# Moving the softmax scaling behind the value product in a pipelined one-core attention and expert kernel

## The reference, cut to what matters

```python
t = t + attn(ln(t))      # softmax(mask(q k^T * C**-0.5)) v, heads side by side, @ Wp + bp
t = t + ffn(ln(t))       # top 2 of 4 experts, gelu(x w1 + b1) w2 + b2, weighted
```

## Time and profile before

| | |
|---|---|
| median of 3 runs | 470.88 us (469.58, 470.88, 472.49) |
| span of the profiled execution | 469.8 us, 1.1 us under the median |
| mean granted TensorE clock | 0.959 of full speed |
| busy: PE, DVE, ACT, POOL | 429.3, 269.8, 263.7, 146.5 us |
| steady block (1 to 6) | 44.2 us each |

### The profile page before, as it was taken

One profiled execution on the slowest core, in us unless ns is written; L12 is line 12 of the kernel. 1 busy time (PEld: TensorE's weight loads), 2 busy tenths in 40 slices (PEclk: granted clock), 3 DMA queues, 4 the chain that ended last, 5 costly groups with the idle time before them and its releaser, 6 DMA issues.

```text
span 469.8 us, 10623 instructions
## 1 busy us (share of the span) xinstructions
PE 429.3 (91%) x3112; PEld 344.1 (73%) x3112; DVE 269.8 (57%) x954; ACT 263.7 (56%) x740; POOL 146.5 (31%) x309
## 2 busy tenths in 40 slices
PE   6999995449779999999999999999999999999897
PEld 6989994325558767877787787778767877787676
DVE  3888887445523853585277527743763586267424
ACT  2444453236557556664866485568556664866370
POOL 5000000235521542254236215531543254235200
PEclk9999998557979999999999999999999999999999
DMA  8500000031021002100210121012002100210000
GB/s 201 130 0 0 0 0 0 17 71 32 3 57 29 19 0 59 44 17 14 66 38 0 38 51 28 0 46 52 19 0 54 46 0 4 76 22 3 7 11 17
DMA packets 14392, 14.93 MB, mean 32 GB/s; under 512 B 5426, under 2 KB 11412, under 8 KB 14372
## 3 DMA queue, kind: packets, MB, share of 16 engines
q1 hardware_dynamic: 14180, 14.30, 12.1%
q0 software_dynamic: 192, 0.39, 0.3%
HBM read 3.86 MB, written 1.57 MB: 12 GB/s over the span
## 4 chain that ended last, share of the span: by engine, by line
PE 73%; DVE 12%; ACT 5%; issue 5%; SPq 2%; DMA 1%; POOL 1%; DVEq 1%; ACTq 0%; POOLq 0%
PE F L1018 18%; PE T L976 9%; PE A L997 8%; PE F L1034 4%; PE F L1038 4%; PE S L960 4%; PE F L1035 4%; PE S L962 3%; PE F L1014 3%; PE S L965 2%; DVE c L629 2%; DVE ig L627 2%; ACT tc_sb L471 2%; DVE pt_sb L457 1%; PE M L939 1%
## 5 line engine op out<-in xcount | busy, mean ns | idle before, releaser
L406 POOL TENSOR_SCALAR p_sb<-p_sb,rden 128x128 f32<-128x128 f32 (+1 forms) x192 | 79.8, 431 | 135.0 <-DVE rden L710 132.8
L1018 PE MATMUL F<-w_sb,hid 128*128 128x96 f32 x768 | 101.0, 276 | 0.0
L1018 PEld LDWEIGHTS F<-w_sb,hid 128*128 128x128 f32 x768 | 93.4, 192 | 6.0 <-issue 6.0
L518 ACT ACTIVATE p_sb<-S,nmax 128x128 f32<-128x128 f32 (+1 forms) x192 | 78.9, 425 | 17.1 <-DVE nmax L704 17.0
L704 DVE TENSOR_REDUCE nmax<-S 128x2 f32<-128x512 f32 (+1 forms) x80 | 50.7, 634 | 52.7 <-PE S L965 52.3
L457 ACT COPY pt_sb<-T 128x512 f32<-128x512 f32 (+1 forms) x48 | 26.4, 550 | 68.7 <-PE T L976 68.7
L564 ACT ACTIVATE hid<-F,b_sb 128x512 f32<-128x512 f32 x72 | 49.3, 686 | 9.6 <-PE F L1038 9.0
L997 PE MATMUL A<-pt_sb,v_cur 128*32 128x128 f32 x576 | 44.2, 284 | 8.5 <-ACT pt_sb L457 4.5
L976 PE MATMUL T<-id_sb,p_sb 128*128 128x128 f32 x288 | 49.2, 290 | 1.5 <-POOL p_sb L406 1.4
L960 PE MATMUL S<-k_bd,q_st 96*128 96x384 f32 (+2 forms) x96 | 39.3, 416 | 6.5 <-DMA k_bd<-k_cur 6.4
L976 PEld LDWEIGHTS T<-id_sb,p_sb 128*128 128x128 f32 x288 | 30.9, 143 | 16.3 <-issue 13.9
(11 more groups left out here) (140 smaller groups left out, 781.8 us busy)
## 6 DMA issues: line engine op xcount, KB each, us to landing
k_bd<-k_cur SPq DMA_DIRECT2D x96, 32.0 KB, 2.0
q_st<-q_cur SPq DMA_DIRECT2D x28, 96.0 KB, 2.2
k_bd<-k_cur SPq DMA_DIRECT2D x96, 16.0 KB, 1.8
t_st<-t_cm SPq DMA_DIRECT2D x7, 192.0 KB, 2.4
out_y<-y_sb SPq DMA_DIRECT2D x7, 192.0 KB, 1.9
x_pad<-in_x SPq DMA_DIRECT2D x2, 612.0 KB, 8.6
w_sb<-in_w SPq DMA_DIRECT2D x1, 576.0 KB
hid<-in_w SPq DMA_DIRECT2D x1, 576.0 KB, 6.9
```

Source lines behind the costliest of these rows:

```text
L406: last = nc.gpsimd.tensor_scalar(p, p, rden[:, u % 3, i:i + 1], 1.0, ALU.mult, ALU.mult)
L518: last = nc.scalar.activation(p_sb[:, u % 3, i * nk:(i + 1) * nk], S[u % 2][:, i * nk:(i + 1) * nk], ACT.Exp, bias=nmax[:, u % 3, i:i + 1] ...
L1018: last = mm(dst[:, e * C:(e + 1) * C], hid[:, c, s * TT:(s + 1) * TT], w2_sb[:, c], start=False, stop=(c == NCH - 1), skip_group_check=True)
```

## The change

The probabilities stay unscaled. The sums of a query tile's six heads are gathered in den[:, s % 2, :] and inverted once a tile (`recip(n, s)`). POOL spreads the six inverses of a row over 16 columns each (`spread`, 128 x 96); PE multiplies that by the identity (`turn_sums`, an fp32 product into bank M, [96, 128]); ACT copies it to rden_t (`take_spread`); and DVE's `heads_out` writes o_t = A * rden_t. project_out(s) and the uses of M are moved ahead of values in PE's round, EARLY_T0 goes from 1 to 4 and EARLY_XT from 4 to 9.

```diff
-EARLY_T0, EARLY_XT = 1, 4
+EARLY_T0, EARLY_XT = 4, 9
...
-            def scale(n, u):
-                wait_alone(pool, rden_done, NU * n + u + 1)
...
-                for i in range(HG[t]):
-                    p = p_sb[:, u % 3, i * nk:(i + 1) * nk]
-                    last = nc.gpsimd.tensor_scalar(p, p, rden[:, u % 3, i:i + 1], 1.0, ALU.mult, ALU.mult)
-                last.then_inc(scaled, 1)
+            def spread(n, s, first=False):
+                wait_alone(pool, rden_done, 4 * n + s + 1)
+                if s or not first:
+                    wait_alone(pool, spread_ready, 4 * n + s)
+                nc.gpsimd.tensor_copy(rden_c[:], rden[:, s % 2].unsqueeze(2).to_broadcast((128, HEADS, HS))
+                                      ).then_inc(rden_spread, 1)
...
-                scale(n, 0)
                 for j in range(NU):
-                    if j + 1 < NU:
-                        scale(n, j + 1)
+                    for s in range(SPB):
+                        if j + 1 == TILE_END[s]:
+                            spread(n, s, first)
                     if j == EARLY_T0 + 1 and not last:
                         rstd1(n + 1)
...
-            def heads_out(n, s, first=False):
-                act.wait_ge(av_ready, NU * n + TILE_END[s])
-                if s or not first:
-                    act.wait_ge(proj_ready, 4 * n + s)
-                nc.scalar.copy(o_t[:], A[0:C, 0:TT]).then_inc(ot_done, 1)
+            def take_spread(n, s, first=False):
+                act.wait_ge(spread_ready, 4 * n + s + 1)
+                if s or not first:
+                    act.wait_ge(ot_done, 4 * n + s)
+                nc.scalar.copy(rden_t[:], M[0:C, 0:TT]).then_inc(spread_done, 1)
...
                         if j == TILE_END[s]:
-                            heads_out(n, s, first)
+                            take_spread(n, s, first)
+                    if j == EARLY_XT and not last:
+                        take_x1(n + 1)
                     if j in PT_ON_ACT:
                         take_pt(act, n, j, first)
                     if j + 2 < NU:
                         exps(n, j + 2, first)
                     if j == EARLY_T0 and not last:
                         take_t0(n + 1)
-                    if j == EARLY_XT and not last:
-                        take_x1(n + 1)
...
+            def heads_out(n, s, first=False):
+                dve.wait_ge(av_ready, NU * n + TILE_END[s])
+                if s or not first:
+                    dve.wait_ge(proj_ready, 4 * n + s)
+                dve.wait_ge(spread_done, 4 * n + s + 1)
+                V.tensor_tensor(o_t[:], A[0:C, 0:TT], rden_t[:], ALU.mult).then_inc(ot_done, 1)
...
-                    if j + 1 < NU:
-                        recip(n, j + 1)
+                    for s in range(SPB):
+                        if j + 2 == TILE_END[s]:
+                            recip(n, s)
+                        if j == TILE_END[s]:
+                            heads_out(n, s, first)
                     if j not in PT_ON_ACT:
                         take_pt(dve, n, j, first)
-                    if j == EARLY_XT + 1 and not last:
+                    if j == EARLY_XT and not last:
                         x1_rest(n + 1)
...
             def probs_t(n, u, first=False):
-                pe.wait_ge(scaled, NU * n + u + 1)
+                pe.wait_ge(exp_done, NU * n + u + 1)
...
+            def turn_sums(n, s, last=False):
+                if s == 1 and not last:
+                    pe.wait_ge(t0_done, n + 2)
+                elif s == SPB - 1 and not last:
+                    pe.wait_ge(x1lo_done, n + 2)
+                elif s:
+                    pe.wait_ge(t1_done, 4 * n + s)
+                else:
+                    pe.wait_ge(v_done, n + 1)
+                if s == SPB - 1:
+                    pe.wait_ge(t1_done, 4 * n + s)
+                pe.wait_ge(rden_spread, 4 * n + s + 1)
+                mm(M[0:C, 0:TT], rden_c[:].rearrange("p r d -> p (r d)"), id_sb[:], start=True, stop=True
+                   ).then_inc(spread_ready, 1)
...
+                        for s in range(SPB - 1):
+                            if j == TILE_END[s]:
+                                turn_sums(n, s, last)
+                            if j == TILE_END[s] + 1:
+                                project_out(n, s)
+                        if j == EARLY_T0 and not last:
+                            pe.wait_ge(t1_done, 4 * n + 1)
+                            tokens_first(n + 1)
+                        if j == EARLY_XT and not last:
+                            pe.wait_ge(t1_done, 4 * n + 3)
+                            channels_first(n + 1)
                         values(n, j - 1, first)
...
                     project_q(n + 1)
+                turn_sums(n, SPB - 1, last)
                 values(n, NU - 1, first)
```

More of the change, by code:

```diff
@@ L136, in hybrid_kernel @@
         nmax = sb("nmax", [128, 3, HG[0]])
-        den = sb("den", [128, 3, HG[0]])
-        rden = sb("rden", [128, 3, HG[0]])
+        den = sb("den", [128, 2, HEADS])
+        rden = sb("rden", [128, 2, HEADS])
+        rden_c = sb("rden_c", [128, HEADS, HS])
+        rden_t = sb("rden_t", [C, TT])
         p_sb = sb("p_sb", [128, 3, 512])
@@ L197, in hybrid_kernel @@
         av_ready = sem("av_ready")
+        spread_ready = sem("spread_ready")
+        spread_done = sem("spread_done")
+        rden_spread = sem("rden_spread")
         proj_ready = sem("proj_ready")
@@ L235, in hybrid_kernel @@
         comb = sem("comb")
-        scaled = sem("scaled")
         rs1_step = sem("rs1_step")
@@ L280, in as_f32, with row_of @@
             return ap.bitcast(F32)
+        def row_of(h):
+            return 2 * (h % 3) + h // 3
         def queries_taken(eng, n, g):
@@ L397, in residual @@
                                         ALU.add).then_inc(tb_done, 1)
-            def scale(n, u):
-                wait_alone(pool, rden_done, NU * n + u + 1)
-                _, t, _ = UNITS[u]
-                nk = TT * (t + 1)
-                for i in range(HG[t]):
-                    p = p_sb[:, u % 3, i * nk:(i + 1) * nk]
-                    last = nc.gpsimd.tensor_scalar(p, p, rden[:, u % 3, i:i + 1], 1.0, ALU.mult, ALU.mult)
-                last.then_inc(scaled, 1)
+            def spread(n, s, first=False):
[4 more added lines that the diff above has]
+                                      ).then_inc(rden_spread, 1)
             def x1_whole(n):
@@ L514, in exps @@
                     act.wait_ge(pt_ready, NU * n + u - 2)
-                _, t, _ = UNITS[u]
+                a, t, h0 = UNITS[u]
+                s = 2 * a + t
+                if h0 == 0 and (s > 1 or not first):
+                    act.wait_ge(rden_done, 4 * n + s - 1)
                 nk = TT * (t + 1)
@@ L519, in exps @@
                                                 ACT.Exp, bias=nmax[:, u % 3, i:i + 1],
-                                                accum_out=den[:, u % 3, i:i + 1])
+                                                accum_out=den[:, s % 2, row_of(h0 + i):row_of(h0 + i) + 1])
                 last.then_inc(exp_done, 1)
-            def heads_out(n, s, first=False):
-                act.wait_ge(av_ready, NU * n + TILE_END[s])
+            def take_spread(n, s, first=False):
+                act.wait_ge(spread_ready, 4 * n + s + 1)
                 if s or not first:
-                    act.wait_ge(proj_ready, 4 * n + s)
-                nc.scalar.copy(o_t[:], A[0:C, 0:TT]).then_inc(ot_done, 1)
+                    act.wait_ge(ot_done, 4 * n + s)
+                nc.scalar.copy(rden_t[:], M[0:C, 0:TT]).then_inc(spread_done, 1)
             def body(n, first=False, last=False):
@@ L545, in body @@
                         take_t0(n + 1)
-                    if j == EARLY_XT and not last:
-                        take_x1(n + 1)
-                heads_out(n, SPB - 1, first)
+                take_spread(n, SPB - 1, first)
                 if not last:
@@ L705, in row_max, with recip @@
                                 AX.X, ALU.max, negate=True).then_inc(max_done, 1)
[L707 to L710, removed]
+            def recip(n, s):
+                dve.wait_ge(exp_done, NU * n + TILE_END[s])
+                V.reciprocal(rden[:, s % 2], den[:, s % 2]).then_inc(rden_done, 1)
+            def heads_out(n, s, first=False):
[4 more added lines that the diff above has]
+                V.tensor_tensor(o_t[:], A[0:C, 0:TT], rden_t[:], ALU.mult).then_inc(ot_done, 1)
             def attn_residual(n, s, first=False):
@@ L784, in body @@
                     route(n - 1, 1)
-                recip(n, 0)
                 if first:
@@ L812, in body @@
                             normalize2(n, s)
+                heads_out(n, SPB - 1, first)
                 attn_residual(n, SPB - 1)
@@ L1054, in body @@
                     probs_t(n, j, first)
[L1055 to L1075, removed]
                 if not last:
@@ L1081, in body @@
```

(1 more changed line is left out.)

## The result

The changed kernel takes 499.91 us (median of 4 runs, 498.56 to 500.96) against 471.15 (4 runs, 469.58 to 472.49): ratio 1.0603, 95% interval 1.0573 to 1.0634. The profiled execution is the shortest of the four, span 496.7 us. A launch takes about 1.8 us over its span in both kernels (498.56 and 496.7 here; 471.54 and 469.7 in a run of the kernel before).

The account below looks back on a forecast made before the run. TensorE's written order was taken to bound the kernel from block 1 on. Steady blocks 18.4, block 7 0.5 and block 0 2.5 us on the 469.8 span gave 491.2, plus 1.1: 492.3 us, range 486 to 498 (8 in 10: 477 to 503).

Parts of the forecast that it names:

- Bound by TensorE's order, scaling hidden: From block 1 on TensorE's order sets the pace; POOL's scaling is hidden, so removing it can only pay in block 0.
- First wait: Steady block, j = 5: TensorE at turn_sums(1) waits 0.86 us for ACT's copy to t0.
- Second wait: Steady block, j = 7: turn_sums(2) waits 1.75 us for t1 of attn_residual(1), which stands behind normalize1 on DVE.
- Turns: TensorE gets 32 turn_sums at 0.2 us each: 0.8 us a block, 6.4 in all, bounds 4.8 to 7.0.
- Steady term: Blocks 1 to 6 each grow by 3.07 us, from 44.2 to 47.3: 18.4 us in all.
- step 1: Walk of the steady block at j = 4: tokens_first replaces channels_first; probs_t(4) starts at about 205.85, j = 5 at 206.33.
- Block 0: First block: loses POOL's scaling but gets both waits larger, +2.5 us, bounds 0 and +5.
- Block 7's +0.5: Last block, without t0 or normalize1 in the way: 0.8 us of work, part in old waits, so +0.5.
- The clock rival: TensorE may drop to 1.2 GHz in steady blocks, 3 us a block more: 500 to 513 us; chance 0.13.
- Launch around the span: The median of the runs lies 1.1 us over the span, carried over from 491.2 to 492.3 us.
- only work: First rival listed: new waits hidden, some 0.45 us a block added; 472 to 484 us, middle 477; chance 0.15.
- faster: Block 0 loses POOL and DVE links (-4 us), turns fit in steady blocks' old waits (-2.1): 465 us; chance 0.06.

Follow-up runs that it names:

- e5: The kernel before with the softmax scaling left out (no reciprocals on DVE, no multiplies on POOL): 469.22 us, ratio 0.9952.
- e2: The changed kernel with take_t0 put ahead of the exponentials of unit 6 on ACT in round 4: 496.42 us.
- e1: The changed kernel with attn_residual put ahead of norm1 and normalize1 in each of DVE's rounds: 491.58 us.
- e7: e1 with POOL's spread of query tile 2 also one round earlier, ahead of rstd1: 488.53 us.
- e3: The changed kernel with take_t0 as in e2, the spread as in e7, attn_residual as in e1, and normalize1 a round later: 478.93 us, ratio 1.0204.
- e4: The changed kernel with each product of turn_sums issued twice, the second over the first: 507.27 us.
- e8: The changed kernel with ten products that nothing reads issued in block 0 ahead of turn_sums(2), where TensorE otherwise waits: 496.36 us.

## Why the prediction was right, and where it was off

The time lies in the range (477 to 503), the forecast's own 486 to 498 was missed by 2 us, and the growth was 28.8 us where 21.4 were forecast. Step by step, in us from the start of the stretch (189.49 before, 198.15 after):

| start of | forecast | measured |
|---|---|---|
| probs_t(4) | 16.36 | 16.52 |
| turn_sums(1) | 19.11 | 19.35 |
| values(4) | 19.36 | 19.74 |
| turn_sums(2) | 25.16 | 25.46 |
| values(7) | 27.21 | 27.63 |
| project_q | 30.26 | 30.82 |
| project_out(3) | 32.76 | 33.21 |

- **Bound by TensorE's order, scaling hidden.** Right: e5 shows 44.22 us with no scaling at all, and block 0 gives the 2 us.
- **First wait, 0.86 us by t0.** Right in place and releaser; 0.94 as listed, 1.1 from start to start, and e2 took it away and won 1.05.
- **Second wait, 1.75 us by attn_residual behind normalize1.** Right in place, releaser and size (1.53 as listed, 1.7 from start to start). What I did not see is that behind DVE's order stand POOL's (e1) and, once that is mended, heads_out(2) (e7): with M's users in their new places, three queues have to be changed together. e1 alone won 1.02; all together (e3) won 2.37 of the 3.53 us. Of the 1.16 left, 0.86 are the turns (e4).
- **Turns, 0.2 us each.** Right (0.215 in e4). The Trainium skill, page "TensorE: Matmul & The Clock Gate", section "LDWEIGHTS (loading the stationary operand)", would have 80 ns for one load of 96 columns; the trace has 163 ns as the median of these fp32 loads, so that rule does not hold here, while two of them, overlapped with the products, come at the distance of the transposes.
- **Steady term, 3.07 us a block.** Mis-sized: 3.53, in six blocks 2.8 us. A third of it is a slip in step 1: its own terms (+0.2 - 0.28 + 0.28) put probs_t(4) at 206.00, not 205.85, that is at 16.51 from the start of the stretch, where 16.52 was measured; all that follows stood 0.15 too early. The timeline shows the rest: a turn that had to wait takes 0.39 us from its start to the next product's (217.50 to 217.89), and I had counted 0.25, twice; t0's end to the turn's start is 0.13 us, counted as 0.05; project_q comes 0.73 us after probs_t(9), before 0.41, so it waits longer for x1lo than the 0.2 that I gave it. Other pieces came out 0.2 us shorter than walked.
- **Block 0, +2.5 us, bounds 0 and +5.** Mis-sized: +5.45, over its upper bound. The waits in it, 1.51 and 2.33 us, are larger than in the steady blocks, as forecast. The step that failed is the clock: the middle value kept it at its old course, and it fell once more behind the second wait. e8 prices that at 2.7 us; without it the term would be +2.8. Block 7's +0.5 was right (+0.57).
- **The clock rival (0.13).** Not as I had it: the profiled execution has a clock of 1.00 in all steady stretches, and a fall in a steady pass costs 1.3 us where the rival charged 3. The three others have a mean clock of 0.948 against its 0.954 and are 1.2 to 2.4 us longer, and e2, e4 and e8 show single steady stretches that are 1.3 us longer at 0.96 to 0.97. That the same happened in those three executions is inferred, as no trace shows them. By the Trainium skill, page "TensorE: Matmul & The Clock Gate", section "A second HAM failure mode: psum-queue depth-cycling", short idle times between groups can make the clock go up and down. The traces agree in part: every fall in a steady pass comes behind the wait of 1.53 us, and those in the last block behind three or four waits of 0.36 to 0.68 us, but 18 of 24 passes with the long wait kept their clock, and the loop of the kernel before, with two waits of 0.44 and 0.48, never lost it.
- **Launch around the span.** I carried 1.1 us; the runs show 1.8: 0.7 of the miss. With 2.8 from the steady blocks, 2.7 from blocks 0 and 7 and the earlier start, and 1.35 by which the median lies over the profiled execution, that is the distance from 492.3 to 499.91.
- **Rivals "only work" and "faster".** Both out: the new waits were there, and with them removed (e3) the added work alone kept the kernel 2% slower. The 478.93 is close to the 477 of the first rival, but by luck in part: its own sum (470.9 + 3.6 - 1.4) gives 473, as it hides 0.35 of the 0.8 us a block in the old waits, and e3's stretches kept 1.16.

## What to carry to other kernels

Before taking a step off an idle engine, remove it altogether on paper: where the steady stretch does not depend on it, the change can only add. When a shared bank's users are moved closer together, walk the order of every engine that empties the bank, and ask on each what stands in its queue ahead of the piece that the next user waits for; mending one queue shows the next. A wait on the bounding engine may cost its clock as well, as that of 2.33 us did in block 0 and that of 1.53 us in 6 of 24 steady passes; so waits of this size can cost more than their length.

## What the runs showed of the hardware that was not expected

The clock of one and the same loop differs from pass to pass: in e2, three of six equal stretches had a time at 1.2 GHz and three had none, 48.0 against 46.7 us. In all traces together, such a fall came only in passes with a wait of 1.53 us (6 of 24; none in 48 passes without a wait over 1 us); why it came in some of them and not in others is left open. Filling one idle time of 2.33 us in block 0 with useless products kept the clock at 2.4 GHz there and made block 0 2.67 us shorter. A turn by transpose (one instruction) in place of an fp32 product by the identity (two) is worth 0.12 us each (0.47 a stretch).
